# Five of seven layer-0 tiles as three passes of rounded operands in a CIN kernel on one Trainium2 core

## The reference, cut to what matters

```python
def _cin_layer(X0, Xi, W, b):            # X0 (512, 39, 16), W (128, 39*Fi)
    Wr = W.reshape(128, 39, Xi.shape[1])
    return jnp.einsum('hjk,bjd,bkd->bhd', Wr, X0, Xi) + b[None, :, None]

e  = stack of 39 table rows per example                   # (512, 39, 16)
x1 = _cin_layer(e, e,  W0, b0)                            # layer 0
x2 = _cin_layer(e, x1, W1, b1)                            # layer 1
x3 = _cin_layer(e, x2, W2, b2)                            # layer 2
z  = concat(x1.sum(2), x2.sum(2), x3.sum(2))              # (512, 384)
h  = relu(concat(z, dense_ctx) @ W_top1 + b_top1)
y  = relu(h @ W_top2 + b_top2) @ W_top3
```

## Time and profile before

| | us |
|---|---|
| median of 3 runs (687.46 to 687.90) | 687.69 |
| the profiled execution, its own time | 687.18 |
| its span, first to last instruction | 685.4 |
| PE busy | 651.5 (95%) |
| DVE busy | 555.4 (81%) |
| ACT busy | 493.8 (72%) |
| POOL busy | 342.5 (50%) |

### The profile page before, as it was taken

How to read it: one execution, slowest core, us unless ns; L and a number is a source line. 1 busy time by engine, 2 the same in 40 slices (tenths; PEclk the granted TensorE clock), 3 DMA queues, 4 the chain that set the end, 5 groups by cost and what they waited for, 6 DMA issues and landing times.

```text
span 685.4 us, 13530 instructions
## 1 busy us (share of the span) xinstructions
PE 651.5 (95%) x2498; PEld 455.9 (67%) x2498; DVE 555.4 (81%) x1211; ACT 493.8 (72%) x1645; POOL 342.5 (50%) x335
## 2 busy tenths in 40 slices
PE   0489999999999999999999999999999999999998
PEld 0166777777777777777777777777777777774443
DVE  0558898989898989999998989898989999996000
ACT  2166878787887878787878787887878788985002
POOL 6778484738383847566564738383843333000000
PEclk9999999999999999999999999999999999999999
DMA  6532613131312222130303132322222030001000
GB/s 217 130 101 63 223 39 92 39 88 42 88 42 80 52 60 70 39 86 16 99 22 95 36 87 43 87 43 80 50 61 66 29 87 5 0 17 61 1 0 0
DMA packets 40750, 43.44 MB, mean 63 GB/s; under 512 B 20224, under 2 KB 23680, under 8 KB 40585
## 3 DMA queue, kind: packets, MB, share of 16 engines
q1 hardware_dynamic: 24354, 39.60, 19.4%
q0 software_dynamic: 5120, 1.32, 2.1%
q10 hardware_dynamic: 11239, 2.05, 1.6%
HBM read 41.62 MB, written 1.31 MB: 63 GB/s over the span
## 4 chain that ended last, share of the span: by engine, by line
PE 87%; DVE 4%; issue 3%; POOL 2%; DMA 1%; ACT 1%; DVEq 0%; SPq 0%; ACTq 0%
PE acc L359 14%; PE ya L382 12%; PE ya L383 11%; PE ya L384 11%; PE yd L382 9%; PE yd L384 8%; PE yd L383 8%; PE yd L456 5%; PE misc L366 4%; DVE chain L498 2%; POOL emb L304 2%; PE misc L352 1%; DVE x2t L513 1%; DMA x<-x_rows 1%; PE ya L470 1%
## 5 line engine op out<-in xcount | busy, mean ns | idle before, releaser
L614 ACT ACTIVATE prods<-ya,x0t 128x128 f32<-128x128 f32 x1472 | 442.5, 503 | 103.5 <-PE ya L384 103.1
L498 DVE SCALAR_TENSOR_TENSOR chain<-yd,x0t,chain 128x128 f32<-128x128 f32 x768 | 217.9, 342 | 16.7 <-PE yd L384 16.1
L382 PE MATMUL ya<-w1h,x1h 128*128 128x512 f32 (+1 forms) x384 | 206.5, 538 | 1.9 <-DVE x1l L517 1.9
L233 POOL TENSOR_TENSOR prod<-tiles,x0a 120x512 f32<-120x512 f32 x105 | 137.4, 1308 | 128.7 <-PE acc L359 116.8
L304 POOL DMA_INDIRECT emb<-in_tables,rows x160 | 158.3, 990 | 39.4 <-issue 26.3
L383 PE MATMUL ya<-w1l,x1h 128*128 128x512 f32 (+1 forms) x384 | 148.1, 386 | 0.0
L384 PE MATMUL ya<-w1h,x1l 128*128 128x512 f32 (+1 forms) x384 | 147.7, 385 | 0.0
L513 DVE TENSOR_REDUCE x2t<-prods 128x128 f32<-128x1792 f32 x64 | 129.2, 2018 | 1.5 <-DVE chain L498 0.3
L359 PE MATMUL acc<-prod,w 120*128 120x512 f32 x224 | 116.5, 604 | 0.7 <-POOL prod L233 0.6
L513 DVE TENSOR_REDUCE prods<-prods 128x128 f32<-128x1536 f32 x64 | 111.7, 1745 | 0.0
L382 PE MATMUL yd<-w1h,x1h 128*128 128x512 f32 x256 | 104.4, 408 | 1.6 <-DVE chain L498 0.7
(11 more groups left out here) (61 smaller groups left out, 357.2 us busy)
## 6 DMA issues: line engine op xcount, KB each, us to landing
tiles<-x_rows SPq DMA_DIRECT2D x236, 78.0 KB
x0a<-x_rows SPq DMA_DIRECT2D x45, 80.0 KB
emb<-in_tables,rows POOLq DMA_INDIRECT x160, 2.4
w<-in_w SPq DMA_DIRECT2D x3, 832.0 KB, 10.2
w<-in_w SPq DMA_DIRECT2D x1, 2496.0 KB, 10.8
tiles<-x_rows SPq DMA_DIRECT2D x32, 42.0 KB
x<-x_rows SPq DMA_DIRECT2D x16, 78.0 KB
tiles<-x_rows SPq DMA_DIRECT2D x15, 72.0 KB
```

The source lines that it names most:

```text
L233: engine.tensor_tensor(prod0[:, i % L0_PRODS, :], tiles[:, slot, :], x0a[:, :], ALU.mult).then_inc(prod0_ready, 1)
L382: pe.matmul(out, x1h[:, xs], w1h[:, cols], start=True, stop=False)
L498: dve.scalar_tensor_tensor(out, product, x, run if step else b1[:, :], ALU.mult, ALU.add).then_inc(yd_used, 1)
L614: mm = act.activation(prods[:, :, slot_of(q) + i], ya[(NA * g + k) % YA][:, i * H:(i + 1) * H], ACT.Copy, scale=turned(c)[:, g * F1 + j:g ...
```

## The change

For chunks 2 to 15, layer-0 tiles 0 to 4 become three passes over rounded operands, as layer 1 has them. Once, at the start, ScalarE rounds five tiles of `w0` to `w0h`, and VectorE subtracts to get `w0l`. For each such tile ScalarE rounds the product (`round_product`, 120x512, put at (3,5) of the chunk before for tile 0 and at (0,0), (0,5), (1,0) and (1,5) for tiles 1 to 4), GpSimd subtracts to get the remainder (`split_product`, behind the next product), and TensorE waits for the remainder and runs high by high, low weights by high, high weights by low. Tiles 5 and 6, and all of chunk 1, stay plain float32. A split product's buffer comes free with GpSimd's subtraction; the rounded halves have two buffers each, which come free with the three passes.

GpSimd's block diagonals move to i = 1, 3, 5 and 6, and its ten gathers to 1, 1, 1, 1, 1, 2 and 3 over the seven steps. The output row `y` moves into a buffer of `prod0`.

```diff
@@ -71,7 +71,12 @@
 L0_AFTER = ((0, 3), (0, 8), (1, 3), (1, 8), (2, 3), (2, 8), (3, 1))
 L0_AFTER_0 = ((1, 3), (1, 6), (1, 9), (2, 2), (2, 5), (2, 8), (3, 1))
 G_AFTER, TURN_1 = 6, (0, 8)
-DIAG_AFTER = {0: 0, 2: 1, 4: 2, 6: 3}
+DIAG_AFTER = {1: 0, 3: 1, 5: 2, 6: 3}
+GATHERS_AFTER = (1, 1, 1, 1, 1, 2, 3)
+
+SPLIT, SPLIT_FROM = (0, 1, 2, 3, 4), 2
+HIGH_AFTER = {0: (3, 5), 1: (0, 0), 2: (0, 5), 3: (1, 0), 4: (1, 5)}
+assert sum(GATHERS_AFTER) == FO
 
 
 def lay_after(prev):
@@ -105,6 +110,30 @@
     if i >= ring:
         return T0 * x + i - ring + 1
     return 0 if isinstance(x, int) and x == 0 else T0 * (x - 1) + range(i, T0, ring)[-1] + 1
+
+
+def splits_before(x, k):
+
+    return len(SPLIT) * (x - SPLIT_FROM) + k
+
+
+def products_free(x, i):
+
+    if i >= L0_PRODS:
+        px, pi = x, i - L0_PRODS
+    else:
+        px, pi = x - 1, range(i, T0, L0_PRODS)[-1]
+    if px >= SPLIT_FROM and pi in SPLIT:
+        return "split", splits_before(px, SPLIT.index(pi)) + 1
+    return "plain", T0 * px + pi + 1
+
+
+def halves_free(x, i):
+
+    k = SPLIT.index(i)
+    if k >= L0_PRODS:
+        return T0 * x + SPLIT[k - L0_PRODS] + 1
+    return T0 * (x - 1) + SPLIT[range(k, len(SPLIT), L0_PRODS)[-1]] + 1
 
 
 def wait_done(engine, semaphore, count):
@@ -139,6 +168,10 @@
         x0a = sb("x0a", [K0, COLS])
         tiles = sb("tiles", [K0, L0_TILES, COLS])
         prod0 = sb("prod0", [K0, L0_PRODS, COLS])
+        w0h = sb("w0h", [K0, len(SPLIT), H], F32R)
+        w0l = sb("w0l", [K0, len(SPLIT), H], F32R)
+        prod0h = sb("prod0h", [K0, L0_PRODS, COLS], F32R)
+        prod0l = sb("prod0l", [K0, L0_PRODS, COLS], F32R)
         x1 = sb("x1", [P, COLS])
         x1h = sb("x1h", [P, COLS], F32R)
         x1l = sb("x1l", [P, COLS], F32R)
@@ -154,7 +187,6 @@
         bias2d = sb("bias2d", [P, 1])
         bt1 = sb("bt1", [P, HID1 // P])
         bt2 = sb("bt2", [P, HID2 // P])
-        y = sb("y", [1, B])
 
         w0ab = gram[0:K0, 0:4, :].rearrange("p j b -> p (j b)")[:, 0:2 * T0 * H].rearrange("p (i n) -> p i n", i=2)
         after = prods[:, :, :].rearrange("p h s -> p (h s)")
@@ -164,6 +196,7 @@
 
         wt1_0, wt1d, dense = x1[:, :], x0a[0:DENSE, :], tiles[0:DENSE, 0, :]
 
+        y = prod0[0:1, 0, :]
         h1, h2 = gram[:, 0:4, :], gram[:, 4:6, :]
         scratch = nc.dram_tensor("x0_rows", (CHUNKS, FP, COLS), F32, kind="Internal").ap()
 
@@ -185,6 +218,8 @@
         lay_done, x0_ready = sem("lay_done"), sem("x0_ready")
         scratch_in = sem("scratch_in")
         x0a_in = sem("x0a_in")
+        w0h_ready, w0_split = sem("w0h_ready"), sem("w0_split")
+        prod0_high, prod0_split = sem("prod0_high"), sem("prod0_split")
         prod0_ready, l0_done = sem("prod0_ready"), sem("l0_done")
         x1_ready = sem("x1_ready")
         x1h_front, x1h_back = sem("x1h_front"), sem("x1h_back")
@@ -229,7 +264,8 @@
                 engine.wait_ge(x0a_in, 3 * 16 * (x + 1))
             slot = i % L0_TILES
             engine.wait_ge(tile_in[slot], 16 * SEGMENTS * (x * len(range(slot, T0, L0_TILES)) + i // L0_TILES + 1))
-            wait_done(engine, l0_done, uses_before(i, L0_PRODS, x))
+            kind, count = products_free(x, i)
+            wait_done(engine, prod0_split if kind == "split" else l0_done, count)
             engine.tensor_tensor(prod0[:, i % L0_PRODS, :], tiles[:, slot, :], x0a[:, :],
                                  ALU.mult).then_inc(prod0_ready, 1)
 
@@ -292,7 +328,7 @@
             sp.dma_start(wt1, a["W_top1"][H:3 * H, :].rearrange("(i p) n -> p i n", p=P)).then_inc(mlp_in, 16)
             sp.dma_start(wt2, a["W_top2"].rearrange("(i p) n -> p i n", p=P)).then_inc(mlp_in, 16)
             sp.wait_ge(tail_act, 8)
-            sp.dma_start(a["out"].rearrange("b o -> o b"), y[:, :]).then_inc(out_done, 16)
+            sp.dma_start(a["out"].rearrange("b o -> o b"), y).then_inc(out_done, 16)
             sp.wait_ge(out_done, 16)
 
         @block.gpsimd
@@ -314,6 +350,15 @@
                 mask = const[:, C_MASK:C_MASK + GB].rearrange("p (b o) -> p b o", o=1)
                 pool.tensor_tensor(diag[:, n % 2, :, :], row.to_broadcast([P, GB, F1]),
                                    mask.to_broadcast([P, GB, F1]), ALU.mult).then_inc(diag_ready, 1)
+
+            def split_product(x, i):
+
+                k = SPLIT.index(i)
+                pool.wait_ge(prod0_high, splits_before(x, k) + 1)
+                pool.wait_ge(prod0_ready, T0 * x + i + 1)
+                wait_done(pool, l0_done, halves_free(x, i))
+                pool.tensor_tensor(prod0l[:, k % L0_PRODS, :], prod0[:, i % L0_PRODS, :],
+                                   prod0h[:, k % L0_PRODS, :].bitcast(F32), ALU.subtract).then_inc(prod0_split, 1)
 
             pool.wait_ge(ids_in, 2 * 16)
             base = first_row[:, :].rearrange("p (o f) -> p o f", o=1).to_broadcast([P, CHUNKS, FO])
@@ -330,10 +375,12 @@
                 for i in range(T0):
                     if c + 1 < CHUNKS:
                         multiply0(pool, c + 1, i)
+                        if c + 1 >= SPLIT_FROM and i - 1 in SPLIT:
+                            split_product(c + 1, i - 1)
                     if i in DIAG_AFTER:
                         block_diagonal(c, DIAG_AFTER[i])
-                    if c + 3 < CHUNKS and 2 * i < FO:
-                        gather(c + 3, range(2 * i, 2 * i + 2))
+                    if c + 3 < CHUNKS:
+                        gather(c + 3, range(sum(GATHERS_AFTER[:i]), sum(GATHERS_AFTER[:i + 1])))
 
         @block.tensor
         def _(pe):
@@ -353,11 +400,20 @@
                 mm.then_inc(x0t_done, 1)
 
             def layer0(x, i):
-                pe.wait_ge(prod0_ready, T0 * x + i + 1)
-                if i == 0:
+                first, last = i == 0, i == T0 - 1
+                if first:
                     wait_done(pe, x1_ready, x)
-                pe.matmul(acc0[:, :], w0[:, i, :], prod0[:, i % L0_PRODS, :],
-                          start=(i == 0), stop=(i == T0 - 1)).then_inc(l0_done, 1)
+                if x >= SPLIT_FROM and i in SPLIT:
+                    k = SPLIT.index(i)
+                    high, low = prod0h[:, k % L0_PRODS, :], prod0l[:, k % L0_PRODS, :]
+                    pe.wait_ge(prod0_split, splits_before(x, k) + 1)
+                    pe.matmul(acc0[:, :], w0h[:, k, :], high, start=first, stop=False)
+                    pe.matmul(acc0[:, :], w0l[:, k, :], high, start=False, stop=False)
+                    pe.matmul(acc0[:, :], w0h[:, k, :], low, start=False, stop=last).then_inc(l0_done, 1)
+                else:
+                    pe.wait_ge(prod0_ready, T0 * x + i + 1)
+                    pe.matmul(acc0[:, :], w0[:, i, :], prod0[:, i % L0_PRODS, :],
+                              start=first, stop=last).then_inc(l0_done, 1)
 
             def gram_group(n, g):
                 pe.wait_ge(sums_done, 2 * n + 2)
@@ -424,6 +480,7 @@
                 layer0(0, i)
             pe.wait_ge(x0t_ready, 1)
             lay_out(1)
+            pe.wait_ge(w0_split, 1)
             pe.wait_ge(w1_split, W1_PARTS)
             chunk(0, False, True, True)
             for c in range(1, CHUNKS - 2):
@@ -554,6 +611,9 @@
                                   ALU.subtract).then_inc(w1_split, 1)
             for i in range(T0):
                 multiply0(dve, 0, i)
+            dve.wait_ge(w0h_ready, 1)
+            dve.tensor_tensor(w0l[:, :, :], w0[:, SPLIT[0]:SPLIT[-1] + 1, :], w0h[:, :, :].bitcast(F32),
+                              ALU.subtract).then_inc(w0_split, 1)
             dve.wait_ge(bias_in, 3 * 16)
             split_x1(0, FRONT, x1h_front, x1_front)
             chunk(0, False, True)
@@ -615,12 +675,22 @@
                                         scale=turned(c)[:, g * F1 + j:g * F1 + j + 1])
                 mm.then_inc(ya_used, 1)
 
+            def round_product(x, i):
+
+                k = SPLIT.index(i)
+                act.wait_ge(prod0_ready, T0 * x + i + 1)
+                wait_done(act, l0_done, halves_free(x, i))
+                act.activation(prod0h[:, k % L0_PRODS, :], prod0[:, i % L0_PRODS, :], ACT.Copy).then_inc(prod0_high, 1)
+
             def chunk(c, prev, nxt, lay):
                 split_back(c)
                 for g in range(GROUPS):
                     for q in range(BLOCKS):
                         if OWNERS[q] == "A":
                             multiply(c, g, q)
+                        for i in SPLIT:
+                            if (g, q) == HIGH_AFTER[i] and (lay if i == 0 else prev and nxt):
+                                round_product(c + 1 + (i == 0), i)
                         if lay and (g, q - 2) == lay_after(prev):
                             evacuate_layout(c + 2)
                         if lay and (g, q - 2) == turn_after(prev):
@@ -643,6 +713,8 @@
             for i in range(1, L0_TILES, 2):
                 load_tile(act, 0, i)
             evacuate_x0t(0)
+            act.wait_ge(w0_ready, 1)
```

(3 more changed lines are left out.)

## The result

The changed kernel takes 702.1 us (median of four runs, 699.66 to 704.27) against 687.68 before on the same chip: a ratio of 1.0209, interval 1.0174 to 1.0244. It is 14.4 us slower where 683.0 was forecast. The profiled execution took 701.41 us on a span of 699.6, 14.2 us over the span before. Three stretches make that up, measured between the 384-column x1l subtractions, each of which is made for the chunk that follows: 1.5 us were there at the one for chunk 1, at 78.52 instead of 77.05 (1.3 of them already at the one for chunk 0, 39.55 instead of 38.27); chunk 1 added 4.4 (41.45 instead of 37.03); the 13 chunks behind it added 8.3 (484.94 instead of 476.64, from the subtraction for chunk 2 to the last).

What follows compares the result with a forecast made beforehand. TensorE was taken to bound the kernel, with VectorE 2.7 us behind per chunk. 13 chunks x 0.54 = 7.0 us less 2.35 lost in chunk 1 gave 4.7, so 687.7 became 683.0; range 678 to 688.

Steps and rivals of the forecast that it cites:

- GpSimd's subtraction: Remainders of the split layer-0 tiles on GpSimd: busy 28.4 us per chunk instead of 21.85, hidden, cost nothing.
- rival B: Behind block (0,1), GpSimd holds VectorE's x1l subtraction by b: 13 x (0.54 - b) - 2.35; 685.6 to 700.1 us; chance 0.27.
- Three passes: Each split layer-0 tile on TensorE: 3 x 0.23 replaces 0.86 us, saving 0.17 per tile, 0.85 per chunk.
- 0.54 us of it survive VectorE: Steady chunk: 0.20 us gained ahead of block (1,8) plus 0.34 behind it; bounds 0.34 and 0.85.
- VectorE's wait at group 1: Sign at group 1's first block: VectorE's wait for TensorE falls from 0.37 to 0.17 us.
- TensorE's wait at (1,8): Sign at block (1,8): TensorE's wait for a `yd` buffer grows from 0.28 to about 0.6 us.
- ScalarE's rounding: Five copies per chunk on ScalarE, 0.62 us each, 3.1 in all; cost nothing, 0.1 to 0.2 if cover went.
- Chunk 1: ScalarE waits for chunk 2's late first product, delaying TensorE's layout 3.2 us; less 0.85 gained, a 2.35 us loss.
- The one-off split of w0: At the start, beside chunk 0's layer 0: some 0.9 us each on ScalarE and VectorE; taken as nothing, at most 1.8.
- A: Rival: VectorE does not bind, so all 0.85 us per chunk come, period 35.9, total 679.0 us; chance 0.12.
- D: Rival: VectorE gives nothing at group 1, 0.34 us per chunk, total 685.6 us; chance 0.10.
- C: Rival: ScalarE's wait in chunk 1 is hidden, 14 x 0.54 = 7.6 us gained, total 680.1; chance 0.09.

Runs made afterwards that it cites:

- the moves alone: Kernel before with only the block diagonals and gathers moved to the change's places, no rounded passes; ratio 0.9993, median 690.14 beside 690.06.
- W2 later: Changed kernel with the 2.5 MB load of W2 issued behind chunk 2's loads instead of ahead of them; ratio 1.0152.
- remainder 1 waiting: Changed kernel with GpSimd's subtraction for tile 1 of the next chunk waiting for VectorE's 128-column x1l subtraction; ratio 0.9974, median 688.79 beside 690.04.
- the last experiment: Kernel before with none, one or two dummy GpSimd products behind the first of two gathers after product 1; the 128-column subtraction took 0.28, 1.87, 3.12 us.
- all three edits: Changed kernel with gathers ahead of remainder 1, W2 loaded after chunk 2's tiles, remainder 1 waiting for x1l, block diagonal 0 behind step 1; ratio 0.9921, median 686.03.

## Why the prediction was wrong

**The step that failed** is the one on GpSimd's subtraction: "I take nothing". The prediction asked only when tile 2 needs its remainder. That answer was right; TensorE doesn't wait for it. What the remainder does to the engine beside it was left to rival B, at 0.27, half of it for short blocks. B is what happened, and in its long form: "it runs from about 338.0 to 339.3, and the next subtraction stands right behind it" is the row pair 310.97 and 312.23. With the measured hold of 1.23 us, B's own formula gives 13 x (0.54 - 1.23) = -9.0 for the steady chunks; with the 0.89 of chunks 13 and 14 it gives the 8.3 that were lost. The trace of before gave the place and the order. Its one overlap that was read, 0.13 us with a block diagonal, was called too short to settle it. The kernel with the moves alone shows that it was just that: an overlap of up to 0.14 leaves the 0.55 as it is, one of 0.29 adds 0.17. But "No row here shows such a block" holds only for the rows that the prediction used. Further on, where no gathers are left, the trace of before has a product right behind the subtraction:

```profile
518.11 0.55 DVE L517 TENSOR_TENSOR x1l<-x,x1h 128x384 fp32r<-128x384 f32 x1
...
518.20 1.62 POOL L233 TENSOR_TENSOR prod<-tiles,x0a 120x512 f32<-120x512 f32 x1
```

VectorE came first there, by 0.09 us, and GpSimd's product took 1.62 us; the one at 554.92, in the same place, took 1.61, where a product has 1.31 on average. So the two engines could be seen to hold each other, and the step should have carried the price. The rule that was weighed there (the Trainium skill, SBUF — State Buffer, section Who interferes with whom) agrees with the runs in this: two-input subtraction against GpSimd's reads, 0.63 to 1.87 us; against fills, 0.28. That the order of issue decides cannot be read from the starts in a trace: a GpSimd operation queued behind another goes ahead of the subtraction that started before it (two products, 1.87 us; product behind a gather, 1.87). When the queued operation was issued, no run here shows.

**Three passes**: right, 0.23 us apart where 0.86 stood.

**0.54 us of it survive VectorE**: right, and hidden by the hold. With the hold gone a chunk takes 36.20 us, 0.53 less than 36.73. VectorE's wait at group 1 fell from 0.37 to 0.20 (0.17 forecast). One sign came only in part: counted by the distance between starts, as in the prediction, TensorE's wait at (1,8) grew from 0.28 to 0.45 us, not to 0.6. Another 0.14 stands around the Gram product of group 0 (302.97), which was not forecast. The added 0.17 and this 0.14 make the 0.31 us that the prediction lost at (1,8) alone.

**ScalarE's rounding**: 0.685 us instead of 0.62, close to where it was to meet VectorE's sum; no wait of that sum shows, and 36.20 leaves no room for one.

**Chunk 1**: the mechanism was right, the size too small. A loss of 2.35 us was forecast, 4.4 came. The layout was 5.0 us late (84.64 instead of 79.65), of which 1.5 were there before the chunk, so the stop is 3.5 against 3.2. The rest is what follows a stop: the lower clock, some 0.2 us on each of eight passes, and a held subtraction of 0.68.

**The one-off split of w0** was put at nothing to 1.8 us. The 1.5 us ahead of chunk 1 lie within that, but the same stretch differs by as much among kernels with the same split (77.35 with W2 later, 78.77 with remainder 1 waiting). The subtraction for chunk 0 starts at 38.27 to 39.01 us in the four kernels without the split and at 37.87 to 39.55 in the eight with it, so this term stays open.

**The other rivals**: A (35.9 us a chunk) and D (36.4) fall with 36.20, C falls with ScalarE's 4.02 us.

## What to carry to other kernels

Before work is given to an idle GpSimd, list VectorE's instructions with two inputs in SBUF and see what GpSimd will be running, or have queued, at each: such an instruction can become as long as that queue, however short it is itself. Idle time on GpSimd is free only where no such instruction stands beside it, or where GpSimd is made to wait for it; one wait gave back 13.6 us here. A stop of TensorE can cost more than its own length: behind the ones of 3.36 and 2.55 us here the next passes were slower, too.

## What was not expected of the hardware

GpSimd operations that read SBUF, in a row, keep VectorE's two-input subtraction out until the last has ended (0.28 us becomes 1.87 with two products in a row, 3.12 with two behind a gather), while fills and gathers alone leave it at 0.28.

TensorE's granted clock fell after it had been idle 3.36 us (0.50 in the next full stretch) and, in the last experiment, 2.55 us (busy times by stretch, first the idle stretch, then the one behind it):

```profile
238.00:241.00 3.00, 0.47 (x3) 0.42 (x3) 3.00 (x5) 0.79 (x4) 2.60 (x3) 1.00 0.12 29
241.00:244.00 3.00, 3.00 (x9) 2.09 (x8) 3.00 (x7) 2.45 (x9) 2.09 (x3) 0.59 0.31 82
```

A chunk with that stop takes 41.1 us, 4.4 more than one without, though the subtraction is only 2.84 longer. After the idle 1.10 us of each steady chunk of the changed kernel the clock stayed at 1.00, and so it did after the 2.08 us ahead of 81.76 in the kernel with all three edits.
